# Attention and feed-forward block on one core: the opening of the kernel laid anew (constants on GpSimd, one bias load, later Wv and Wp loads, wide weight splits)

## The chip, the core and the metric
One core of one Trainium2 chip runs the whole kernel. The metric is the device time of one launch in microseconds. The kernel before takes 2347.75 us (median of 3 runs, 2345.22 to 2349.53).

## What is computed
`x` is 4 x 2048 x 512 in f32, split below into units of 512 tokens.

```
x = x + layernorm(attn(layernorm(x)))     # 16 heads of 32, causal, every 4th key is masked out
x = x + layernorm(ffn(layernorm(x)))      # one of 8 matrices, chosen by argmax(log_softmax(logits) + gumbel(u))
attn: q, k, v = y @ Wq + bq, y @ Wk + bk, y @ Wv + bv;  softmax(q k / sqrt(32)) v;  @ Wp + bp
```

Matrices and rows go through TensorE as two f16 halves each (a high part, and a low part that holds what the high part lost), with power-of-two scales taken from the largest weight, so that a projection is three f16 products for every 128 rows of the contraction.

## The kernel before
**Units.** There are 16 units (4 sequences x 4 blocks of 512 tokens). A unit normalises four row blocks (r = 0 to 3, 128 rows each), turns them by a DMA transpose, projects q, k and v, and then goes through four groups g of four heads: the largest score of each query ("peak", on DVE), its transfer into the scores as a shift, scores, exponentials (ACT), values ("pv") and sums. Then come the output projection, its norm, the feed-forward projection and its norm.

**Order.** Nothing is scheduled on the chip. The class `Order` gives each engine (PE, ACT, DVE, GpSimd, SP) a list of steps before the program is built. Each step has a rank, a duration in ns, the steps that it needs and the banks or buffers that it takes; a planner runs them forwards and backwards several times and keeps the shortest plan. An engine works through its own list strictly in order, and stands still at a step that waits for a semaphore. A changed duration, need or rank in `startup` can so move steps anywhere in the program, in all 16 units.

**The opening** (`Order.startup`, and the engine blocks of `sandwich_block`):

- SP loads (`load_w`, L738) and the row blocks (`load_x`, L719): Wk, x0, x1, Wq, x2, x3, Wv, a table of masks, Wp and the output bias, in that order. x0 to x2 take 2 or 3 transfers each, since their rows are gathered by keys that are kept and keys that are not. `turn` (L734) is the DMA transpose of a row block. `kcopy` (L753) copies two constant rows of KST to the other three key blocks.
- ACT's list begins with `load_b` (L846 to L853): logits, u, the identity matrix, then eight loads for bq and bk (128 values each) and one for bv. Then it normalises (L886, L888) and casts (L894) row blocks. `kconst` (L866) writes 2^15 into rows 96 and 97 of KST (2 x 6144 f16). `choose` (L857 to L863) is the Ln, Ln, Exp, Ln by which the feed-forward matrix is chosen; each change of function comes with a table load. `whigh` (L875) writes the high f16 part of Wq and Wk: for each column block of 128 and each of four 128-row blocks k one instruction that also reorders the columns within the block (a head's 32 columns are spread 4 apart), so 32 instructions in all. `wlow` (L1169) does the same on DVE for the low part, 32 more. Wv, Wp and the chosen matrix are split by one instruction each (128 x 2048, L879 and L1176).
- DVE: `consts` (L981 to L987), `stats` of each row block (L1020 to L1025), `wmax` (largest weight, L1096), `bmax` (L1103), then `allmax` and `scales` (L1109 to L1162: with two small matmuls on PE, L1259 and L1263, they give each matrix its scale). `fold` 0 and 1 bring bv through Wp into the output bias, `fold` 2 (L1191 to L1208, 17 instructions) cuts both biases into three bf16 rows. The output projections and the v evacuations of unit 1 wait for `fold` 2.
- GpSimd: `rstd` (L803, the inverse root), `low` (L810, low part of a row block), `rest` (L815, low part of q or k).

A first projection on PE (L1247 to L1249) needs the two split halves of its column block and all four turned row blocks.

Of the kernel before, what the change touches and what calls it, by code (L numbers as in the profile page):

```python
# [52 lines left out]
class Order:  # L53
# [69 lines left out]
    def startup(self):  # L123
        add = self.add
        add("dve", -100, 1200, ("consts",))
        add("act", -100, 7500, ("load_b",))
        for i, n in enumerate((1, 0, 2, 3)):
            add("sp", -101 if n == 1 else -99 + i, (650, 650, 1300, 1300)[i], ("load_w", n))
            add("hbm", -100 + i, (2100, 2100, 2700, 2900)[i], ("land", n), [("sp", "load_w", n)])
        add("hbm", -101, 2500, ("land", "b"), [("act", "load_b")])  # L130
        add("dve", -97, 200, ("ident",), [("act", "load_b"), ("dve", "consts")])
        add("act", -99, 5400, ("kconst",), [("dve", "consts")])
        add("sp", 0.5, 1950, ("kcopy",), [("act", "kconst")])
# [24 lines left out]
        add("dve", 0.5, 3200, ("fold", 2), [("dve", "fold", 1), ("dve", "wlow", 3), ("dve", "wlow", 4), ("dve", "scales", 2)])  # L158
# [308 lines left out]
def sandwich_block(nc, x, Wq, bq, Wk, bk, Wv, bv, Wp, bp, Wf, bf, logits, uni, cf, cb, out):  # L467
# [21 lines left out]
    with ctx:  # L489
# [42 lines left out]
        WX = sb("WX", [8, 1], F32)  # L532
        WD = sb("WD", [8, 8], F32)
# [26 lines left out]
        a_p, a_k, a_w, a_n, a_c, a_h, a_e, a_o, a_m, a_q, a_v, a_y = (  # L560
            sem(n) for n in ("a_p", "a_k", "a_w", "a_n", "a_c", "a_h", "a_e", "a_o", "a_m", "a_q", "a_v", "a_y"))
        v_p, v_c, v_w, v_f, v_ln, v_n, v_m, v_s, v_o, v_t = (
            sem(n) for n in ("v_p", "v_c", "v_w", "v_f", "v_ln", "v_n", "v_m", "v_s", "v_o", "v_t"))
        g_ln, g_p, g_q, g_s, g_o, g_r = (sem(n) for n in ("g_ln", "g_p", "g_q", "g_s", "g_o", "g_r"))
# [16 lines left out]
        BIAS = 9 * 16  # L581

        def counted(steps, signals):

            total, value = {}, {}
            for s in steps:
                name, n = signals(s)
                if n:
# [9 lines left out]
                                           {"load_b": (None, 0), "choose": ("p", 4), "kconst": ("k", 1),  # L598
                                            "whigh": ("w", 4 if s[0] == "whigh" and s[1] < 2 else 1), "exp": ("e", 1),
# [3 lines left out]
            "allmax": ("p", 2), "scales": ("p", (16, 12, 6)[s[-1]] if s[0] == "scales" else 0), "wlow": ("w", 4 if s[0] == "wlow" and s[1] < 2 else 1),  # L603
# [3 lines left out]
            "rstd": ("ln", 1), "low": ("p", 1), "rest": ("q", 1), "add": ("s", 1),  # L607
# [89 lines left out]
        def _(e):  # L697
# [6 lines left out]
            for s in order.sp:  # L704
# [45 lines left out]
                elif kind == "kcopy":  # L750
                    sp.wait_ge(a_k, 1)
# [89 lines left out]
        def _(e):  # L841
            ac = Lean(e)
            for s in order.act:
                kind = s[0]
                if kind == "load_b":
                    e.dma_start(g8(0), logits[None, :]).then_inc(d_lg, 16)  # L846
                    e.dma_start(g8(1), uni[None, :]).then_inc(d_lu, 16)
                    e.dma_start(IDF, cf).then_inc(d_cf, 16)
                    for n, b in enumerate((bq, bk)):
                        for k in range(4):  # L850
                            e.dma_start(BIA[:, n, k:k + 1], b[128 * k:128 * k + 128].rearrange("(a d) -> d a", a=4),
                                        allow_slow_non_contiguous=True).then_inc(d_b, 16)
                    e.dma_start(BIA[:, 2, :], bv.rearrange("(k p) -> p k", p=128),  # L853
                                allow_slow_non_contiguous=True).then_inc(d_b, 16)
# [9 lines left out]
                elif kind == "kconst":  # L864
                    ac.wait_ge(v_c, READY)
                    e.activation(KST[96:98, :, 0:384],  # L866
                                 ONES[96:98, 0:1].rearrange("p (a n) -> p a n", a=1).broadcast_to([2, H, 384]),
                                 ACT.Copy, scale=SM).then_inc(a_k, 1)
# [103 lines left out]
        def _(e):  # L972
# [5 lines left out]
            for s in order.dve:  # L978
# [184 lines left out]
                elif kind == "wlow":  # L1163
                    n = s[1]
                    if n < 2:
                        c = slice(128 * s[2], 128 * s[2] + 128)
                        for k in range(4):
                            dv.wait_ge(a_w, AC["whigh", n, s[2]] - 3 + k)
                            e.scalar_tensor_tensor(out=WL[:, n, k, c].rearrange("p (d a) -> p a d", a=4),  # L1169
                                                   in0=stage[n][:, k, c].rearrange("p (a d) -> p a d", a=4),  # L1170
                                                   scalar=SW[:, n:n + 1],
                                                   in1=WH[:, n, k, c].rearrange("p (d a) -> p a d", a=4),
                                                   op0=ALU.mult, op1=ALU.subtract).then_inc(v_w, 1)
# [38 lines left out]
        def _(e):  # L1212
            pe = Lean(e)
            for s in order.pe:
# [72 lines left out]
                elif kind == "score":  # L1287
# [4 lines left out]
                    pe.wait_ge(a_k, 1)  # L1292
# [37 lines left out]


_INS = ['L0_attn_x', 'L0_attn_Wq', 'L0_attn_bq', 'L0_attn_Wk', 'L0_attn_bk', 'L0_attn_Wv', 'L0_attn_bv',
        'L0_attn_Wp', 'L0_attn_bp', 'L0_ffn_W', 'L0_ffn_b', 'L0_ffn_logits', 'L0_ffn_u']


# [33 lines left out]
```

## Time and profile before

| what | value |
|---|---|
| three runs | 2345.22, 2347.75, 2349.53 us |
| the profiled execution | 2347.21 us |
| its span on the core | 2345.4 us |
| PE busy | 2255.9 us, 96% |
| ACT, DVE, GpSimd busy | 1739.0, 1629.9, 1553.1 us |
| mean granted TensorE clock | 0.99 |

The span is what the trace covers; the execution's own time is 1.8 us more. A granted clock of 1.00 is 2.4 GHz, 0.50 is 1.2 GHz. Busy shares are means over the span, and the opening is 2 to 5% of it.

### The profile page before, as it was taken

What the parts mean: (1) busy time and instruction counts of PE and PEld (TensorE: products, weight loads), DVE (VectorE), ACT (ScalarE), POOL (GpSimd) and SP (SyncE); (2) the same over time, 40 slices, a digit from 0 to 9 for tenths busy, and PEclk for the clock granted to TensorE, in tenths of its full rate; (3) what the DMA queues carried; (4) which work ended last, traced back from release to release, by engine and by line L of the source; (5) the groups of instructions that cost most, each with busy time, mean ns of one, the idle gap of its engine ahead of it and who ended that gap; (6) DMA issues with size and microseconds to landing.
All of it is one profiled execution on the core that took longest, in us unless ns stands there. A gap on an engine that the chain in (4) does not pass through costs nothing.

```text
span 2345.4 us, 43402 instructions
## 1 busy us (share of the span) xinstructions
PE 2255.9 (96%) x14996; PEld 960.0 (41%) x14996; DVE 1629.9 (69%) x4773; ACT 1739.0 (74%) x3206; POOL 1553.1 (66%) x1440
## 2 busy tenths in 40 slices
PE   4799999999999999999999999999999999999996
PEld 2344443443444444443344444443344444444422
DVE  8768667775477777677366777777727677767774
ACT  7568678688777868678876867868777686776773
POOL 3246587688655758688854747868965476777734
PEclk9899999999999999999999999999999999999998
DMA  7313122012233213112133412201223231310101
GB/s 195 79 40 91 32 51 72 17 42 69 53 96 83 59 29 70 49 40 66 39 70 81 92 31 61 67 23 36 62 56 91 61 91 30 62 49 24 35 10 41
DMA packets 224358, 137.49 MB, mean 59 GB/s; under 512 B 146730, under 2 KB 196618, under 8 KB 224138
## 3 DMA queue, kind: packets, MB, share of 16 engines
q1 hardware_dynamic: 222310, 134.65, 23.3%
q8 instruction: 118, 1.93, 0.4%
q14 instruction: 102, 0.84, 0.1%
q10 hardware_dynamic: 1828, 0.07, 0.1%
HBM read 39.69 MB, written 16.78 MB: 24 GB/s over the span
## 4 chain that ended last, share of the span: by engine, by line
PE 69%; issue 8%; DVE 7%; POOL 7%; ACT 6%; DMA 1%; SPq 1%; POOLq 0%; ACTq 0%; DVEq 0%
PE acc L1276 12%; PE acc L1312 11%; PE acc L1296 11%; PE acc L1247 9%; PE acc L1248 8%; PE acc L1249 8%; PE acc L1327 6%; POOL P L824 5%; ACT P L962 4%; PE acc L1300 2%; DVE acc L1039 2%; DVE STA L1020 1%; PE acc L1252 1%; DVE MP L1043 1%; DMA XB<-in_L_attn_x_dram 1%
## 5 line engine op out<-in xcount | busy, mean ns | idle before, releaser
L962 ACT ACTIVATE P<-acc,EX 128x512 f32<-128x512 f32 (+2 forms) x1920 | 1076.7, 639 | 229.7 <-PE acc L1300 100.2
L824 POOL TENSOR_TENSOR P<-P 128x512 f32<-128x512 f32 x732 | 907.4, 1277 | 112.8 <-PE acc L1312 86.6
L1043 DVE TENSOR_REDUCE MP<-acc 128x1 f32<-128x512 f32 (+1 forms) x1088 | 720.0, 680 | 210.3 <-PE acc L1276 206.8
L1039 DVE CUSTOM_DVE_ANT_0 acc<-acc,CB 128x96 f32<-128x96 f32 (+7 forms) x1024 | 450.8, 456 | 244.6 <-PE acc L1276 240.0
L1276 PE MATMUL acc<-KST,QST 96*128 96x512 f16 (+9 forms) x2112 | 594.6, 334 | 13.2 <-DVE MP L1039 4.5
L1296 PE MATMUL acc<-QST,KST 98*128 98x512 f16 (+2 forms) x1920 | 581.4, 354 | 15.8 <-DVE MP L1039 7.2
L1312 PE MATMUL acc<-P,V 128*32 128x512 f32 (+2 forms) x3840 | 430.5, 543 | 2.4 <-ACT P L962 2.2
L1276 PEld LDWEIGHTS acc<-KST,QST 96*128 96x128 f16 x2112 | 196.8, 98 | 302.1 <-issue 56.8
L1296 PEld LDWEIGHTS acc<-QST,KST 98*128 98x128 f16 x1920 | 182.5, 98 | 287.5 <-issue 75.2
L803 POOL TENSOR_TENSOR RR<-RR,NHALF 128x1 f32<-128x1 f32 x256 | 143.1, 563 | 202.9 <-DVE NM L1025 202.5
L1327 PE MATMUL acc<-P,ONES 128*32 128x512 f32 (+2 forms) x2304 | 231.8, 501 | 1.7 <-ACT P L962 1.6
L815 POOL TENSOR_TENSOR QKL<-SC,QKH 128x384 f16<-128x384 f32 (+1 forms) x128 | 134.7, 1052 | 136.5 <-ACT QKH L937 136.5
L1247 PE MATMUL acc<-XT,WH 128*128 128x384 f16 (+1 forms) x512 | 182.3, 356 | 12.9 <-DVE WL L1169 11.3
L1249 PE MATMUL acc<-XT,WH 128*128 128x384 f16 (+1 forms) x512 | 181.3, 354 | 0.0
L1248 PE MATMUL acc<-XT,WL 128*128 128x384 f16 (+1 forms) x512 | 181.2, 354 | 0.0
L1312 PEld LDWEIGHTS acc<-P,V 128*32 128x32 f32 x3840 | 102.8, 109 | 184.2 <-issue 145.1
L1300 PE MATMUL acc<-CB 128*128 128x176 bf16 x768 | 176.1, 241 | 0.0
L828 POOL TENSOR_TENSOR OTL<-SC,OTH 128x512 f16<-128x512 f32 x64 | 74.3, 1161 | 144.3 <-ACT OTH L969 144.0
L1039 DVE DVE_READ_ACCUMULATOR2_ANT MP<- 128x1 f32 x1024 | 144.6, 141 | 0.0
L1327 PEld LDWEIGHTS acc<-P,ONES 128*32 128x32 f32 x2304 | 70.4, 109 | 134.5 <-issue 113.5
L886 ACT ACTIVATE NM<-NM,RR 128x1 f32<-128x1 f32 x244 | 72.1, 296 | 71.1 <-POOL RR L803 67.5
L1076 DVE STREAM_TRANSPOSE SC<-acc 128x512 f32<-128x512 f32 x64 | 45.7, 714 | 112.3 <-PE acc L1327 112.3
(151 smaller groups left out, 2896.9 us busy)
## 6 DMA issues: line engine op xcount, KB each, us to landing
QST<-QKH SPq DMA_DIRECT2D x128, 128.0 KB, 3.2
XR<-in_L_attn_x_dram SPq DMA_DIRECT2D x60, 256.0 KB, 2.7
out_dram<-XR SPq DMA_DIRECT2D x60, 256.0 KB, 2.2
KST<-QKH SPq DMA_DIRECT2D x128, 96.0 KB, 2.7
XB<-in_L_attn_x_dram SPq DMA_DIRECT2D x48, 252.0 KB
QST<-QKL SPq DMA_DIRECT2D x64, 128.0 KB, 3.3
KST<-QKL SPq DMA_DIRECT2D x64, 96.0 KB, 2.7
XB<-in_L_attn_x_dram SPq DMA_DIRECT2D x20, 256.0 KB, 3.4
```

Source lines behind the costliest of these rows:

```text
L824: e.tensor_tensor(P[:, acc, a, :], P[:, acc, a, :], P[:, buf, a, :], ALU.add).then_inc(g_s, 1)
L962: e.activation(P[:, p_buf[u, g, sb_], a, t0:512], bank(*step)[:, t0:512], ACT.Exp, scale=EX[:, 1:2]).then_inc(a_e, 1)
L1039: e.tensor_tensor_reduce(out=ps, in0=ps, in1=MASKM[:, 512 - n:512], scale=1.0, scalar=-3.0e38, op0=ALU.add, op1=ALU.max, accum_out=maxima( ...
L1043: e.tensor_reduce(maxima(u, g)[:, r, a, ci:ci + 1], bank(*s)[:, 0:n], AX.X, ALU.max).then_inc(v_m, 1)
L1247: e.matmul(o, lh, rh, start=kt == 0, stop=False)
L1248: e.matmul(o, ll, rh, start=False, stop=False)
L1249: i = e.matmul(o, lh, rl, start=False, stop=kt == 3 and bias is None)
L1276: i = e.matmul(bank(*s)[:, 0:n], QST[0:96, h, 128 * r:128 * r + 128], KST[0:96, h, c0:c0 + n], start=True, stop=True)
L1296: i = e.matmul(bank(*s)[:, t0:512], KST[0:98, h, 128 * sb_:128 * sb_ + 128], QST[0:98, h, t0:512], start=True, stop=dg < 0)
L1300: i = e.matmul(bank(*s)[:, t0:t0 + MW], IDB, MASKT[dg], start=False, stop=True)
L1312: i = e.matmul(bank("pv", u, g, 0)[32 * a:32 * a + 32, t0:512], V[:, vb, 32 * h:32 * h + 32], P[:, p_buf[u, g, sb_], a, t0:512], start=fir ...
L1327: i = e.matmul(bank("sum", u, g, blocks[0])[32 * a:32 * a + 32, t0:512], ONES[:, :], P[:, buf, a, t0:512], start=sb_ == blocks[0], stop=sb ...
```

## The change
The planner's table of the opening gets new durations and needs, and the code follows it:

- The constant rows of KST are written by GpSimd, as the first step of its list, by one memset. SP's `kcopy` and PE's scores wait for GpSimd's semaphore.
- The host lays the biases out as one 128 x 3 x 4 array, and Wq and Wk with their columns already reordered. ACT issues 4 loads where it issued 12, the identity first. A one-element activation after them makes the first table load come early.
- Loads of Wv and Wp (and what goes with them) wait in SP's list until all four row blocks of unit 0 are turned.
- `whigh` and `wlow` of Wq and Wk take one instruction for each column block (128 x 4 x 128), 8 + 8 in place of 32 + 32.
- `fold` 2 is planned at 8500 ns, not at 3200.

```diff
     def startup(self):
-        add("act", -100, 7500, ("load_b",))
+        add("act", -100, 2700, ("load_b",))
         for i, n in enumerate((1, 0, 2, 3)):
-            add("sp", -101 if n == 1 else -99 + i, (650, 650, 1300, 1300)[i], ("load_w", n))
+            add("sp", -101 if n == 1 else -99 + i, (650, 650, 1300, 1300)[i], ("load_w", n),
+                [("sp", "turn", 1, 0, r) for r in range(4)] if n > 1 else [])
-        add("act", -99, 5400, ("kconst",), [("dve", "consts")])
-        add("sp", 0.5, 1950, ("kcopy",), [("act", "kconst")])
+        add("gp", -101, 5400, ("kconst",))
+        add("sp", 0.5, 1950, ("kcopy",), [("gp", "kconst")])
-                add("act", at + m, 1170, ("whigh", n, m), [("dve", "scales", 0)])
-                add("dve", at + m, 1140, ("wlow", n, m), [("act", "whigh", n, m)])
+                add("act", at + m, 620, ("whigh", n, m), [("dve", "scales", 0)])
+                add("dve", at + m, 640, ("wlow", n, m), [("act", "whigh", n, m)])
-        add("dve", 0.5, 3200, ("fold", 2), ...)
+        add("dve", 0.5, 8500, ("fold", 2), ...)
...
@@ gpsimd
-                if kind == "rstd":
+                if kind == "kconst":
+                    e.memset(KST[96:98, :, 0:384], SM).then_inc(g_k, 1)
+                    gp.wait_ge(g_k, 1)
+                elif kind == "rstd":
@@ scalar, load_b
+                    e.dma_start(IDF, cf).then_inc(d_cf, 16)
+                    e.dma_start(BIA[:, :, :], bias).then_inc(d_b, 16)
                     e.dma_start(g8(0), logits[None, :]).then_inc(d_lg, 16)
                     e.dma_start(g8(1), uni[None, :]).then_inc(d_lu, 16)
-                    e.dma_start(IDF, cf).then_inc(d_cf, 16)
-                    for n, b in enumerate((bq, bk)):
-                        for k in range(4):
-                            e.dma_start(BIA[:, n, k:k + 1], b[...].rearrange("(a d) -> d a", a=4), ...)
-                    e.dma_start(BIA[:, 2, :], bv.rearrange("(k p) -> p k", p=128), ...)
+                    ac.wait_ge(v_c, 1)
+                    e.activation(WARM[:, :], ONES[:, 0:1], ACT.Identity)
@@ scalar, whigh (wlow on DVE likewise)
-                        for k in range(4):
-                            e.activation(WH[:, n, k, c].rearrange("p (d a) -> p a d", a=4),
-                                         stage[n][:, k, c].rearrange("p (a d) -> p a d", a=4), ACT.Copy,
-                                         scale=SW[:, n:n + 1]).then_inc(a_w, 1)
+                        e.activation(WH[:, n, :, c],
+                                     stage[n][:, :, c], ACT.Copy,
+                                     scale=SW[:, n:n + 1]).then_inc(a_w, 1)
@@ kernel, on the host
+    for n, name in enumerate(('L0_attn_bq', 'L0_attn_bk')):
+        bias[:, n, :] = inputs[name].reshape(4, 4, 32).transpose(2, 1, 0).reshape(128, 4)
+    bias[:, 2, :] = inputs['L0_attn_bv'].reshape(4, 128).T
+        if name in ('L0_attn_Wq', 'L0_attn_Wk'):
+            a = a.reshape(512, 4, 4, 32).transpose(0, 1, 3, 2).reshape(512, 512)
```

**Where the lists move.** ACT's list from its 7th row, before. Line 886 is the first norm, 866 `kconst`, 875 the 32 splits; `choose` (857 to 863) stands after them:

```order
L886 ACT_TABLE_LOAD
L886 ACTIVATE NM<-NM,RR 128x1
L888 ACTIVATE XB<-XB,NM,RR 128x512
L894 ACTIVATE XP<-XB 128x512
L866 ACTIVATE KST<-ONES 2x16x384
```

The same place in the changed kernel, where 855 is the one-element activation, 858 to 864 are `choose` and 881 is the first norm:

```order
L855 ACT_TABLE_LOAD
L855 ACTIVATE WARM<-ONES 128x1
L858 ACT_TABLE_LOAD
L858 ACTIVATE XR<-XR 1x8
L860 ACTIVATE XR<-XR 1x8
L862 ACT_TABLE_LOAD
L862 ACTIVATE XR<-XR 1x8
L864 ACT_TABLE_LOAD
L864 ACTIVATE XR<-XR 1x1
L881 ACTIVATE NM<-NM,RR 128x1
```

The choice of the feed-forward matrix moved ahead of all four norms, and `kconst` left ACT.

SP's list after the first loads of x, before (738 to 742 the weights, masks and output bias, 734 the transposes, 753 `kcopy`):

```order
L738 DMA P<-in_L_attn_Wv_dram 128x4x512
L740 DMA CB<-in_cb_dram 128x1168
L738 DMA V<-in_L_attn_Wp_dram 128x4x512
L742 DMA V<-in_L_attn_bp_dram 128x512
L734 DMA_TRANSPOSE XT<-XP 128x8x128
L719 DMA XB<-in_L_attn_x_dram 126x1x512
L719 DMA XB<-in_L_attn_x_dram 2x512
L753 DMA KST<-KST 2x16x384 x3
L734 DMA_TRANSPOSE XT<-XP 128x8x128
L719 DMA XB<-in_L_attn_x_dram 1x512
```

And now, from the load of Wq on (739 the weights, 735 the transposes, 754 `kcopy`):

```order
L739 DMA P<-in_L_attn_Wq_dram 128x4x512
L754 DMA KST<-KST 2x16x384 x3
L735 DMA_TRANSPOSE XT<-XP 128x8x128
L720 DMA XB<-in_L_attn_x_dram 126x1x512
L720 DMA XB<-in_L_attn_x_dram 2x512
L735 DMA_TRANSPOSE XT<-XP 128x8x128
L735 DMA_TRANSPOSE XT<-XF 128x8x128 x2
L739 DMA P<-in_L_attn_Wv_dram 128x4x512
L741 DMA CB<-in_cb_dram 128x1168
L739 DMA V<-in_L_attn_Wp_dram 128x4x512
```

The four transposes stand closer together and ahead of Wv and Wp, the wait for the constants stands ahead of all four, and the eight transfers of x stand ahead of Wk and Wq but for the last of them.

DVE's list where `fold` 2 begins, before (1039 is a peak of group 1, 1191 to 1208 are `fold` 2):

```order
L1039 ISA acc,MP<-acc,CB 128x192
L1039 ISA MP 128x1
L1191 RECIPROCAL RC<-CO 128x2
L1198 TENSOR_SCALAR V<-V,RC 65x512
L1202 CAST R<-V 1x512
```

And in the changed kernel (1047 to 1054 close the peaks of group 2, 1185 on is `fold` 2; 1084, the output of group 0, follows its last row):

```order
L1047 TENSOR_REDUCE acc<-MP 128x16
L1052 TENSOR_SCALAR MHL<-acc 128x4x4
L1054 SCALAR_TENSOR_TENSOR MHL<-acc,MHL 128x4x4
L1185 RECIPROCAL RC<-CO 128x2
L1192 TENSOR_SCALAR V<-V,RC 65x512
```

`fold` 2 moved behind the peaks of groups 1 and 2. All other lists are laid anew too, through all 16 units, with the same kinds of steps.

## Rows read from the trace of the kernel before

**Rows 1.** The page: busy time of each engine, and the granted clock in 40 slices

```profile
PE 2255.9 (96%) x14996; PEld 960.0 (41%) x14996; DVE 1629.9 (69%) x4773; ACT 1739.0 (74%) x3206; POOL 1553.1 (66%) x1440
PEclk9899999999999999999999999999999999999998
```

**Rows 2.** Stretches: length, busy of PE, PEld, DVE, ACT, POOL, clock, DMA share, GB/s

```profile
5.00:10.00 5.00, 0.00 (x0) 0.00 (x0) 2.13 (x5) 0.31 (x1) 0.56 (x1) 1.00 1.08 307
...
80.00:87.00 7.00, 0.97 (x4) 0.26 (x3) 6.50 (x17) 0.69 (x1) 0.00 (x0) 0.50 0.33 76
87.00:100.00 13.00, 12.58 (x99) 6.61 (x98) 11.35 (x55) 9.33 (x19) 3.41 (x4) 0.76 0.36 63
...
200.00:2200.00 2000.00, 1982.85 (x13286) 845.89 (x13288) 1389.11 (x4072) 1514.53 (x2798) 1410.17 (x1299) 1.00 0.23 56
```

**Rows 3.** Timeline of PE: start, length, what [idle before <-releaser]

```profile
31.22 0.48 PE L1247 MATMUL acc<-XT,WH 128*128 128x384 f16 x1 [11.30 <-DVE WL L1169]
...
86.68 0.61 PE L1296 MATMUL acc<-QST,KST 98*128 98x512 f16 x1 [6.03 <-DVE MP L1039]
```

**Rows 4.** Timeline of ACT in the opening

```profile
9.69 1.28 ACT L886 ACT_TABLE_LOAD   x1 [9.69 <-POOL RR L803]
...
12.81 5.32 ACT L866 ACTIVATE KST<-ONES 2x6144 f16<-2x6144 f32 x1
...
18.16 0.29 ACT L886 ACTIVATE NM<-NM,RR 128x1 f32<-128x1 f32 x1
...
19.87 0.28 ACT L886 ACTIVATE NM<-NM,RR 128x1 f32<-128x1 f32 x1
...
23.25 9.64 ACT L875 ACTIVATE WH<-P,SW 128x128 f16<-128x128 f32 x32
...
36.50 1.28 ACT L857 ACT_TABLE_LOAD   x1
...
41.17 0.20 ACT L863 ACTIVATE XR<-XR 1x1 f32<-1x1 f32 x1
```

**Rows 5.** Timeline of DVE in the opening

```profile
14.45 0.69 DVE L1020 BATCH_NORM_STATS2 STA<-XB 128x6 f32<-128x512 f32 x1
...
15.51 2.28 DVE L1096 TENSOR_REDUCE WM<-P 128x1 f32<-128x2048 f32 x1
...
20.16 1.12 DVE L976 TENSOR_SCALAR PW<-WMA 128x2 int32<-128x2 int32 x1
...
25.12 0.15 DVE L1162 TENSOR_SCALAR EX<-EX 128x1 f32<-128x1 f32 x1
...
42.09 0.17 DVE L976 TENSOR_SCALAR PW<-WMA 128x2 int32<-128x2 int32 x1
...
48.18 2.34 DVE L1176 SCALAR_TENSOR_TENSOR WL<-P,SW,WH 128x2048 f16<-128x2048 f32 x1
```

**Rows 6.** Chain of waits: DVE's first four splits of Wk

```profile
26.34 1.27 DVE WL L1169 x4
```

**Rows 7.** Timeline of GpSimd: a low part

```profile
20.10 1.15 POOL L810 TENSOR_TENSOR XP<-XB,XP 128x512 f16<-128x512 f32 x1 [3.94 <-ACT XP L894]
```

**Rows 8.** Timeline of SP: how long it issues loads of x and transposes

```profile
1.27 3.43 SPq L719 DMA_DIRECT2D XB<-in_L_attn_x_dram  x5
...
5.20 1.83 SPq L719 DMA_DIRECT2D XB<-in_L_attn_x_dram  x3
...
26.41 2.61 SPq L734 DMA_TRANSPOSE XT<-XF  x2
```

**Rows 9.** DMA issues of the first 30 us: KB each, median us to landing

```profile
V<-in_L_attn_Wp_dram SPq DMA_DIRECT2D x1, 1024.0 KB, 11.9
...
YX<-in_cf_dram ACTq DMA_DIRECT2D x1, 64.0 KB, 5.1
...
XT<-XF SPq DMA_TRANSPOSE x2, 3.5
```

**Rows 10.** Timeline of DVE: first and last of the 17 rows of `fold` 2

```profile
76.60 0.16 DVE L1191 RECIPROCAL RC<-CO 128x2 f32<-128x2 f32 x1
...
85.70 0.42 DVE L1202 CAST R<-YX 1x512 bf16<-1x512 f32 x1
```

More of the change, by code:

```diff
@@ L157, in startup @@
         add("dve", 0.3, 600, ("fold", 1), [("pe", "fold"), ("hbm", "land", "b")])
-        add("dve", 0.5, 3200, ("fold", 2), [("dve", "fold", 1), ("dve", "wlow", 3), ("dve", "wlow", 4), ("dve", "scales", 2)])
+        add("dve", 0.5, 8500, ("fold", 2), [("dve", "fold", 1), ("dve", "wlow", 3), ("dve", "wlow", 4), ("dve", "scales", 2)])
     def moments(self, k, u, r, rank, after):
@@ L464, in wait_ge, with sandwich_block @@
             self.seen[sem.name] = value
-def sandwich_block(nc, x, Wq, bq, Wk, bk, Wv, bv, Wp, bp, Wf, bf, logits, uni, cf, cb, out):
+def sandwich_block(nc, x, Wq, Wk, Wv, bias, Wp, bp, Wf, bf, logits, uni, cf, cb, out):
     F32 = mybir.dt.float32
@@ L597, in sandwich_block @@
                                             "f": ("y", 1)}[s[1][0]] if s[0] == "evac" else
-                                           {"load_b": (None, 0), "choose": ("p", 4), "kconst": ("k", 1),
-                                            "whigh": ("w", 4 if s[0] == "whigh" and s[1] < 2 else 1), "exp": ("e", 1),
+                                           {"load_b": (None, 0), "choose": ("p", 4), "whigh": ("w", 1), "exp": ("e", 1),
                                             "ohigh": ("o", 1), "shift": ("m", 1), "high": ("h", 1), "cast": ("c", 1), "norm": ("n", 2)}[s[0]]))
@@ L602, in sandwich_block @@
             "choose": ("p", 4 if s[-1] else 2), "consts": ("c", 7), "ident": ("c", 1), "wmax": ("p", 1), "bmax": ("p", 3),
-            "allmax": ("p", 2), "scales": ("p", (16, 12, 6)[s[-1]] if s[0] == "scales" else 0), "wlow": ("w", 4 if s[0] == "wlow" and s[1] < 2 else 1),
+            "allmax": ("p", 2), "scales": ("p", (16, 12, 6)[s[-1]] if s[0] == "scales" else 0), "wlow": ("w", 1),
             "fold": ("f", 17 if s[-1] == 2 else 1), "stats": ("ln", 4), "norm": ("n", 1),
@@ L606, in sandwich_block @@
         GP = counted(order.gp, lambda s: {
-            "rstd": ("ln", 1), "low": ("p", 1), "rest": ("q", 1), "add": ("s", 1),
+            "kconst": ("k", 1), "rstd": ("ln", 1), "low": ("p", 1), "rest": ("q", 1), "add": ("s", 1),
             "olow": ("o", 1), "add_x": ("r", 1), "add_y": ("r", 1)}[s[0]])
@@ L863, in _ @@
                     e.activation(G8[0:1, 6, 1:2], G8[0:1, 6, 0:1], ACT.Ln).then_inc(a_p, 1)
[L864 to L868, printed above, removed]
                 elif kind == "whigh":
@@ L1166, in _ @@
                         c = slice(128 * s[2], 128 * s[2] + 128)
[L1167 to L1173, printed above, removed]
+                        dv.wait_ge(a_w, AC["whigh", n, s[2]])
+                        e.scalar_tensor_tensor(out=WL[:, n, :, c],
+                                               in0=stage[n][:, :, c],
+                                               scalar=SW[:, n:n + 1],
+                                               in1=WH[:, n, :, c],
+                                               op0=ALU.mult, op1=ALU.subtract).then_inc(v_w, 1)
                     else:
@@ L1348, in give @@
         args.append(nc.dram_tensor(f"in_{name}_dram", a.shape, _mybir.dt.from_np(a.dtype), kind="ExternalInput").ap())
+    bias = _np.zeros((128, 3, 4), _np.float32)
+    for n, name in enumerate(('L0_attn_bq', 'L0_attn_bk')):
+        bias[:, n, :] = inputs[name].reshape(4, 4, 32).transpose(2, 1, 0).reshape(128, 4)
+    bias[:, 2, :] = inputs['L0_attn_bv'].reshape(4, 128).T
     for name in _INS:
-        give(name, _np.ascontiguousarray(inputs[name]))
+        a = bias if name == 'bias' else inputs[name]
+        if name in ('L0_attn_Wq', 'L0_attn_Wk'):
+            a = a.reshape(512, 4, 4, 32).transpose(0, 1, 3, 2).reshape(512, 512)
+        give(name, _np.ascontiguousarray(a))
     BIG = -1.0e38
```

21 lines of the change are left out of this document (9 added, 12 removed).

## The prediction

> **What bounds the kernel now.** I began with the page. PE is busy 96% of the span, at a granted clock near the upper level in every slice [rows 1]. In the 2000 us from 200 to 2200 it is busy 1982.85 us, so 17 us are idle there [rows 2]: in the steady part PE's own work sets the pace. What can be won by touching the opening is therefore the time in which PE has nothing to do at the start, one for one, since whatever starts earlier there lets the same PE work begin earlier.
>
> The timeline of PE shows how much that is. Its first projection starts at 31.22 us, and later it stands 6.03 us before the matmul at 86.68 [rows 3]. The stretches show the second place again: from 80 to 87 us PE is busy 0.97 us, and the granted clock is 0.50, the lower level (1.2 GHz); from 87 to 100 it is still 0.76 [rows 2].
>
> What is waited for at 31.22? The row names DVE's split (L1169), but the first splits of Wk end at 27.61 [rows 6], 3.6 us earlier. The other input is the turned rows: two transposes are issued from 26.41 to 29.02, so the second at about 27.7, and one takes 3.5 us to land [rows 8, 9], which gives 31.2. So the turned rows come last, and the splits would be next, 3.6 us behind them at most. Behind the turned rows stands ACT: after the first cast it writes the constants for 5.32 us, and only at 18.16 does the second norm begin [rows 4].
>
> At 86.68 the cause is `fold` 2: its 17 rows run from 76.60 to 86.12 on DVE [rows 10], and the peaks of group 1 stand behind it. PE's list runs into a peak with no free bank, and the scores that are ready stand behind that peak.
>
> **Term 1, the first projection.** I walk both inputs through the new lists.
>
> *ACT and the rows.* Twelve loads become four. I price the four at 1.75 us of issue from 0.76 us, by the nearest issue rows (SP: 3.43 us for five, 1.83 for three [rows 8], so 0.6 to 0.7 each at most, 2.8 us as the upper end). u is then issued by about 2.5. Its landing is not shown by itself; I take the identity's 5.1 us [rows 9], though that one travelled beside a megabyte of weights, so u is there at 7.6 at the latest. `choose` runs from its first table load to its last activation in 41.37 - 36.50 = 4.87 us [rows 4], so it ends at 12.5; the first table load (1.28 us) that stood at 9.69 is now hidden in the wait for u. A norm with its cast takes 19.87 - 18.16 = 1.71 us, four of them 6.8, so to 19.3. GpSimd's low part adds 1.15 [rows 7], the last transpose goes out at about 20.6 and lands 3.5 later: 24.1. SP is free by then. Its issues of x and two weights are over at about 7 us, the three copies of constants need some 2 us more, the first transpose is due at 15.4, and each takes 1.3.
>
> *DVE and the scales.* About 2.1 MB (x and Wk) must land for the last `stats`, and 3.1 MB with Wq. At 307 GB/s [rows 2], from 1.6 us on, that is 8.4 and 11.7 us; small transfers at the front make it slower, say 10.5 and 14. One `stats` takes 1.06 us (14.45 to 15.51 [rows 5]), so these are done at 11.6. The second part of `choose` on DVE waits for ACT until 12.5 and takes 0.8: 13.3. Two maxima of 2.28 us [rows 5] end at 17.9, with Wq landed well before it is wanted. From the end of the second maximum (17.79) to the end of the scales (25.27) DVE took 7.5 us. Three instructions in it were held up beside GpSimd's low parts: L976 took 1.12 us at 20.16 and 0.17 at 42.09 [rows 5], its second use and a bias scaling were slowed by as much again, and `choose` took 0.3. In the new order the low parts overlap less with this; I subtract the full 3.1 and get 22.3, or 25.4 if nothing changes. One `stats` more: 23.4. The first wide split of DVE: a quarter of the 128 x 2048 split's 2.34 us [rows 5], so 0.6; the upper end is the 1.27 us of four narrow ones [rows 6]. 24.0.
>
> Both inputs come at 24, so **the first projection starts at 24.1 in place of 31.2: 7.1 us.** The ends: 22.5, if u lands in 2 us, and 27, if it lands in 7 or DVE keeps its holds. ACT's splits (9.64 us for 32 [rows 4], now 8 of about 0.6) keep ahead of DVE's.
>
> *Edits that cost nothing.* The memset on GpSimd has no row of its own. The nearest is the same write on ACT, 5.32 us; the ends are 0.5, and 13.8 by a low part's 1.15 us for 512 elements [rows 4, 7]. I take 5.3: it ends at 6, when the first `rstd` is wanted at 6 to 7, and norms wait for `choose` until 12.5 anyway. Without that cover each us past 12 would delay all rows by one. The GPSIMD Engine Reference of the Trainium skill (section 3.1) gives 1.03 to 1.8 cycles for an element in tight loops; an estimate from that page is 5.3 to 9.2 us, and by it the sum would stay as it is. No row shows such a memset.
>
> **Term 2, the rest of the opening.** `fold` 2 now comes after the peaks of groups 1 and 2. While it runs PE holds scores, values and sums of two groups and the projections of unit 1. That removes the wait of 6.03 us and part of the slow clock: 12.58 us busy at 0.76 [rows 2] would be 9.6 at 1.00, so 3 us. Against it, 9.5 us of DVE work do not vanish, and the output of group 0 waits behind them. The ends are a gain of 9 (6 + 3) and a loss of 3.5, if PE stood through all 9.5. **I take 3.5 us of gain**, nearer to the middle of what can be lost or won.
>
> The loads of Wv and Wp start at about 22 us. In PE's list the bias fold with Wp stands after three projections (8.4 us), so at 32.5; 2.4 MB at 307 GB/s land by 30. I cost them at nothing; if Wp took 11.9 us as before [rows 9], it would land at 35.1 and cost 2.6.
>
> **Term 3, all that follows.** The lists of 16 units are laid anew with the same work. I take 0, with 6 us to either side: a third of the 17 us idle of 200 to 2200 [rows 2].
>
> **Sum.** Against the profiled execution's 2347.2 us: 7.1 + 3.5 = 10.6 less, 2336.6. The median of the runs is 0.5 higher, so the forecast is 2337.
>
> **Rivals.**
>
> *Held port (0.07).* The memset is slow and holds what DVE shares with GpSimd. For it speaks the L976 row: 1.12 us against 0.17, and it ended at 21.28, when GpSimd's low part ended at 21.25 [rows 5, 7]. DVE's cast of the identity, second in its new list, would stand until a memset of 13.8 us ends at 14.3. Then 5.9 us of `stats` and small work, 4.6 of maxima, 4.4 of scales, 1.6 to the first split: the first projection at 30.8, term 1 worth 0.4, and the time 2343.8. Against it: ACT wrote the same in 5.32, and with that the cast is free at 6 and the walk above is unchanged. The rule is that of "SBUF — State Buffer" in the Trainium skill, section "Who interferes with whom": whoever issues first gets the shared ports for the whole instruction, and an f32 cast can be such a one. The trace agrees for L976; whether a memset holds them no row shows.
>
> *Won early, given back (0.09).* Late weights cost 2.6, `fold` 2 at its new place takes all of term 2 (3.5), and the q and k spreads, now in the middle of the loads of Wv, Wp and the chosen matrix, land 1.5 us later each at two steps (3). 10.6 - 9.1 leaves 1.5: 2346. For it: the DMA queues ran at a share above 1 from 5 to 10 us [rows 2].
>
> *A worse draw of the order (0.06, slower).* Place: units 2 to 14. PE stands before peaks and scores that wait for DVE and ACT; 17 us in 2000 are little, and another plan may have twice as much or more. It decides from 10.6 us on; at 2.2 times (21 more) the time is 2358. Against it: needs, buffers and all durations outside the opening are as they were.
>
> *More than forecast (0.08).* Term 2 is worth all 9, term 1 as above, a little more behind it: 2331 or below.
>
> **Numbers.** The forecast case has 0.70. A measurement of this kernel can tell about 0.2%, 4.7 us, from no change, so faster means below 2343.0. Faster: 0.70 + 0.08 and a little of the second rival, 0.80. Same: 0.14. Slower: 0.06. The range takes in term 1 from 22.5 to 27, both ends of term 2 in part and term 3: 2328 to 2345.
>
> **What would show it.** Term 1: PE's first L1247 row at 24 (its new line 1241), second norm on ACT at about 14, one table load before 5 us, memset of 5 to 6 us. Term 2: no PE wait over 3 us between 60 and 100, clock above 0.8 there, and `fold` 2 (9.5 us) after the peaks of group 2. Term 3: PE idle from 200 to 2200 of 17 us, give or take 6. The forecast is wrong if the memset is over 12 us, if PE stands at the bias fold, or if that last idle time has grown by 10.

## The result, and the profile after

The changed kernel takes **2334.35 us** (median of 5 runs, 2333.48 to 2335.92), the kernel before 2346.92 in the same comparison (2344.98 to 2349.53). The ratio is 0.9948, with a 95% interval from 0.9933 to 0.9962: faster by 12.6 us, where 10.6 were forecast and 2337 us predicted, within the range. The profiled executions span 2345.4 and 2332.1 us, 13.3 apart.

The page's busy times and granted clock, which answer to [rows 1]:

```profile
PE 2254.5 (97%) x14996; PEld 960.9 (41%) x14996; DVE 1625.2 (70%) x4749; ACT 1729.6 (74%) x3182; POOL 1558.6 (67%) x1441
PEclk9899999999999999999999999999999999999998
```

The stretches, columns as in [rows 2], with two more (31 to 50 and 70 to 80):

```profile
31.00:50.00 19.00, 14.23 (x59) 6.62 (x58) 12.70 (x37) 10.72 (x18) 6.59 (x8) 0.82 0.93 242
...
70.00:80.00 10.00, 8.63 (x38) 4.40 (x38) 8.97 (x52) 6.85 (x11) 2.31 (x2) 0.50 0.33 77
80.00:87.00 7.00, 6.75 (x49) 2.24 (x47) 5.59 (x17) 5.24 (x11) 0.66 (x2) 0.77 0.41 64
87.00:100.00 13.00, 12.52 (x105) 5.90 (x109) 11.67 (x31) 9.40 (x20) 4.16 (x4) 1.00 0.29 78
200.00:2200.00 2000.00, 1982.53 (x13286) 847.23 (x13282) 1386.71 (x4065) 1519.40 (x2803) 1417.89 (x1308) 1.00 0.22 56
```

PE's idle time, length less busy in such stretches, says where the 13.3 us went:

| stretch | before | after |
|---|---|---|
| to the first projection (31.2, 25.3) | 30.0 | 24.1 |
| from there to 200 us | 18.7 | 11.6 |
| 200 to 2200 | 17.15 | 17.47 |
| 2200 to the end | 23.6 | 24.4 |
| PE busy, whole span | 2255.9 | 2254.5 |

So about 6 us came before the first projection, 7 behind it, and the steady part gave and took nothing. PE at three places (it answers to [rows 3]):

```profile
25.26 0.48 PE L1241 MATMUL acc<-XT,WH 128*128 128x384 f16 x1 [4.39 <-DVE WL L1163]
...
45.15 0.42 PE L1270 MATMUL acc<-KST,QST 96*128 96x96 f16 x3 [4.77 <-DMA QST<-QKL]
...
104.12 0.34 PE L1270 MATMUL acc<-KST,QST 96*128 96x384 f16 x1 [1.40 <-DVE SC L1084]
```

Of the wait of 6.03 us nothing is left: from 80 to 87 PE is busy 6.75 us in place of 0.97. The wait at 45.15 is for the spread of the first q (the DMA copies of its high and low part into QST, from which the scores read it; L768); the chain of waits gives it 8.9 us from issue to landing:

```profile
36.21 8.90 DMA QST<-QKL
```

The kernel before had a wait of this kind as well, for the spread of the second q and not of the first:

```profile
59.43 0.24 PE L1276 MATMUL acc<-KST,QST 96*128 96x96 f16 x1 [3.62 <-issue]
```

The row names no releaser, but the same matmul in *e1_wide* (below), which has the same order, does:

```profile
59.64 0.24 PE L1274 MATMUL acc<-KST,QST 96*128 96x96 f16 x1 [4.36 <-DMA QST<-QKL]
```

So the longest wait for a q spread is 4.77 us now and was 3.62: it moved from the second q to the first and grew by 1.2 us.

ACT, as in [rows 4]: the first table load stands at 2.63 us, `choose` ends at 8.99, the first two norms start at 8.90 and 10.60, and seven wide splits take 4.40 us:

```profile
2.63 1.28 ACT L855 ACT_TABLE_LOAD   x1 [2.63 <-issue]
...
8.90 0.28 ACT L881 ACTIVATE NM<-NM,RR 128x1 f32<-128x1 f32 x1
...
21.78 4.40 ACT L870 ACTIVATE WH<-P,SW 128x512 f16<-128x512 f32 x7 [5.54 <-DVE CO L1120]
```

DVE, as in [rows 5]; the first two rows are long and end together, at 6.03 and 6.02, and the later MAX8 is the same instruction on the same shape:

```profile
2.52 3.51 DVE L985 CAST IDH<-YX 128x128 f16<-128x128 f32 x1 [0.47 <-DMA YX<-in_cf_dram]
4.34 1.68 DVE L989 MAX8 XR<-XR 1x8 f32<-1x8 f32 x1
...
12.62 0.69 DVE L1015 BATCH_NORM_STATS2 STA<-XB 128x6 f32<-128x512 f32 x1 [2.93 <-DMA XB<-in_L_attn_x_dram]
...
14.13 0.16 DVE L999 MAX8 XR<-XR 1x8 f32<-1x8 f32 x1
...
14.48 4.45 DVE L1091 TENSOR_REDUCE WM<-P 128x1 f32<-128x2048 f32 x2
...
21.10 0.17 DVE L971 TENSOR_SCALAR PW<-WMA 128x2 int32<-128x2 int32 x1
...
24.38 3.39 DVE L1163 SCALAR_TENSOR_TENSOR WL<-P,SW,WH 128x512 f16<-128x512 f32 x5
...
92.31 0.16 DVE L1185 RECIPROCAL RC<-CO 128x2 f32<-128x2 f32 x1
```

GpSimd's memset, and SP's transposes with what stands around them ([rows 8] had 2.61 us for the last two; now 2.98, all issued by 22.6):

```profile
0.73 5.21 POOL L801 MEMSET KST<- 2x6144 f16 x1 [0.29 <-POOLq L1337]
```

```profile
15.49 1.36 SPq L735 DMA_TRANSPOSE XT<-XP  x1
...
18.33 1.26 SPq L735 DMA_TRANSPOSE XT<-XP  x1
19.64 2.98 SPq L735 DMA_TRANSPOSE XT<-XF  x2
22.66 0.59 SPq L739 DMA_DIRECT2D P<-in_L_attn_Wv_dram  x1
```

### The profile page after: what moved, and what is told of

The parts are those of the page before. It is cut to its first block, busy times and chain, and to the rows that moved or that the text cites. A ratio compares the mean times of both kernels' runs of the same rounds, so it can differ in the third digit from the quotient of the medians.

```text
span 2332.1 us, 43387 instructions
## 1 busy us (share of the span) xinstructions
PE 2254.5 (97%) x14996; PEld 960.9 (41%) x14996; DVE 1625.2 (70%) x4749; ACT 1729.6 (74%) x3182; POOL 1558.6 (67%) x1441
## 3 DMA queue, kind: packets, MB, share of 16 engines
q1 hardware_dynamic: 222310, 134.65, 22.6%
## 4 chain that ended last, share of the span: by engine, by line
PE 72%; issue 7%; POOL 7%; ACT 6%; DVE 6%; DMA 1%; SPq 1%; ACTq 0%; POOLq 0%; DVEq 0%
PE acc L1270 12%; PE acc L1306 12%; PE acc L1290 11%; PE acc L1241 9%; PE acc L1242 9%; PE acc L1243 9%; PE acc L1321 6%; POOL P L828 4%; ACT P L957 3%; PE acc L1294 2%; DVE acc L1034 1%; DVE MP L1038 1%; PE acc L1246 1%; POOL XP L814 1%; POOL RR L807 1%
## 5 line engine op out<-in xcount | busy, mean ns | idle before, releaser
L1290 PE MATMUL acc<-QST,KST 98*128 98x512 f16 (+2 forms) x1920 | 580.9, 354 | 12.6 <-ACT P L957 5.6
L1015 DVE BATCH_NORM_STATS2 STA<-YX 128x6 f32<-128x512 f32 x126 | 86.6, 687 | 31.8 <-ACT YX L921 16.9
```

The lines of the kernel that those rows point to most:

```text
L1290: i = e.matmul(bank(*s)[:, t0:512], KST[0:98, h, 128 * sb_:128 * sb_ + 128], QST[0:98, h, t0:512], start=True, stop=dg < 0)
```

## The experiments

Each run is compared with the kernel before on the same chip; its medians were 2348.16 us beside the four e runs, 2348.84 beside g1_sp, g2_spw, f4_draw and f5_plan3200 (on another chip), 2349.29 beside u1_spback, f2_x3first, f3_spread and h1_both. Where lists are edited, that is done behind the planner's last step, so nothing else moves.

**One part at a time, in the order of before.** *e1_wide*: the wide splits alone.

```diff
-                        for k in range(4):
-                            e.activation(WH[:, n, k, c].rearrange("p (d a) -> p a d", a=4), ...
+                        e.activation(WH[:, n, :, c], stage[n][:, :, c], ACT.Copy, ...
```

> The kernel before with one part of the change: wide splits of Wq and Wk (8 + 8 instructions), every list in the order of before. Theory (the turned rows come last at 31.2 us): PE's first projection stays between 30.7 and 31.5 us, though the first split of Wk ends at 27.0 or earlier; the time stays within 1.5 us of before, 2346.9. Rival (the splits set the start, as the releaser in the row says): first projection at 27 to 28.5, time 3 to 4 us less.

2346.72 us, ratio 0.9992 (0.9983 to 1.0001): no change that can be told from none. Its PE, then its DVE (first wide splits of Wk):

```profile
31.03 0.48 PE L1245 MATMUL acc<-XT,WH 128*128 128x384 f16 x1 [11.23 <-DMA XT<-XF]
```

```profile
25.93 0.74 DVE L1167 SCALAR_TENSOR_TENSOR WL<-P,SW,WH 128x512 f16<-128x512 f32 x1
```

The first split ends at 26.67, 0.9 us earlier than in [rows 6] and 4.4 us ahead of PE, which starts as before: there the turned rows come last, although the row of [rows 3] named the split.

*e2_gpconst*: the memset alone, at the head of GpSimd's list.

```diff
+order.act.remove(("kconst",))
+order.gp.insert(0, ("kconst",))
```

> The kernel before with the KST constants written by a memset at the head of GpSimd's list in place of the 5.3 us activation; all else in the order of before. Theory (ACT's 5.3 us stood in the way of the turned rows): the second norm begins at 12.8 instead of 18.2, the rows are turned by about 26, and the first projection starts at 27.5 to 28 with DVE's narrow split as the new last input, so 3 to 4 us less: 2343 to 2344. Rival (SP's own queue holds the transposes, not ACT): first projection still after 30 us and less than 1 us gained.

2347.15 us, ratio 0.9994 (0.9985 to 1.0003), first projection at 31.20. My theory fell, the rival held. The trace shows why. First GpSimd's low parts, then SP:

```profile
12.54 1.16 POOL L815 TENSOR_TENSOR XP<-XB,XP 128x512 f16<-128x512 f32 x1 [0.17 <-ACT XP L894]
15.76 1.16 POOL L815 TENSOR_TENSOR XP<-XB,XP 128x512 f16<-128x512 f32 x1
...
18.32 1.15 POOL L815 TENSOR_TENSOR XF<-XB,XF 128x512 f16<-128x512 f32 x1 [0.29 <-ACT XF L894]
```

```profile
13.73 3.23 SPq L736 DMA_TRANSPOSE XT<-XP  x1
17.01 1.34 SPq L721 DMA_DIRECT2D XB<-in_L_attn_x_dram  x2
18.40 2.16 SPq L755 DMA_DIRECT2D KST<-KST  x3
20.60 3.23 SPq L736 DMA_TRANSPOSE XT<-XP  x1
23.88 2.01 SPq L721 DMA_DIRECT2D XB<-in_L_attn_x_dram  x3
25.94 3.25 SPq L736 DMA_TRANSPOSE XT<-XF  x2
```

All four rows are ready at 19.5 us, and the last transposes still go out at 25.94: SP issues without a gap from 13.7 on, 5.5 us of it loads and copies that stand between the transposes. Behind the turned rows stood SP's own list. ACT's 5.3 us lay beside it: in the kernel before, SP waited for ACT's late row only from 20.75 to 21.28.

*e3_fold*: `fold` 2 alone, behind the peaks of group 2.

```diff
+order.dve.remove(("fold", 2))
+order.dve.insert(order.dve.index(("peaks", 0, 2)) + 1, ("fold", 2))
```

> The kernel before with the one step fold 2 (17 DVE instructions) moved in DVE's list from within the peaks of group 1 to behind the peaks of group 2, nothing else. Theory (its old place made PE stand 6.0 us at a low clock): no PE wait over 3 us between 76 and 95 us, PE idle between 31 and 120 us falls from 16.9 to 11 or less, and the time falls by 4 to 8 us: 2339 to 2343. Rival (9.5 us of DVE work cost the same wherever they stand): a PE wait of 5 us or more appears near the new place and the time stays within 1.5 us of 2346.9.

2352.57 us, ratio 1.0020 (1.0011 to 1.0029): slightly slower. The wait goes from 86.7 and comes back:

```profile
112.31 0.42 PE L1278 MATMUL acc<-KST,QST 96*128 96x288 f16 x1 [7.59 <-DVE MP L1041]
```

Here `fold` 2 begins at 102.58, and PE, which began its next projections at 99.1, is through with what it can run at 104.7. In the changed kernel `fold` 2 begins at 92.31, and PE has projections, values and sums until 102.7.

*e4_three*: the three edits above together.

> The kernel before with the three parts together (wide splits, constants on GpSimd, fold 2 behind the peaks of group 2), in the order of before otherwise; biases still in nine loads, choice of the matrix late, Wv and Wp loaded early. Theory (opening parts explain the change, the new order of the other units does not): first projection at 25.5 to 27, time 8 to 11 us less than before, 2336 to 2339. Rival (a lucky new order of the 16 units carries the change): 5 us less at most, 2342 or above.

2350.35 us, ratio 1.0010 (1.0001 to 1.0019); first projection at 30.92, waiting for the turned rows again, and the wait of 7.59 us behind `fold` 2 again, at 111.67. The three parts of the change that lie on the engines bring nothing while SP's list and the rest of the order are those of before.

**SP's list.** *g1_sp* is before with the wide splits, the memset, and the copies of constants and three of the four row blocks of unit 1 moved behind the fourth transpose; *g2_spw* moves the loads of Wv and Wp (with the masks and bp) there too.

```diff
+at = order.sp.index(("turn", 1, 0, 3))
+late = [("kcopy",)] + [("load_x", 1, r) for r in (1, 2, 3)]
+late = [("load_w", 2), ("load_w", 3)] + late          # g2_spw only
+late = [s for s in late if order.sp.index(s) < at]
+order.sp[:] = [s for s in order.sp[:at + 1] if s not in late] + late + order.sp[at + 1:]
```

> The kernel before with wide splits and the constants on GpSimd, and in SP's list the constant copies and the loads of x1 to x3 of unit 1 moved behind the fourth transpose; Wv and Wp still loaded early; everything else in the order of before. Theory now (what kept the rows from being turned was SP's own list, where a transpose that is ready stood behind 1.3 to 2.2 us pieces of other issue, and each transpose took 3.2 us to issue while the weights were landing): transposes at 13.7, 18.3, then back to back; last one lands at 25 to 28 us, so the first projection starts at 25 to 28 in place of 31.2. Rival (the landing of Wv and Wp alone holds the transposes up): first projection after 29.

> The same with the loads of Wv, masks, Wp and output bias also behind the fourth transpose. Theory (landing weights lengthen a transpose's issue from 1.3 to 3.2 us): all four issues below 1.7 us, rows turned by 23 us, and the first projection bound by DVE's first split at 24.5 to 25.3, so 6 us earlier than before. For the time: if what is won at the start passes to the end one for one, 2341 to 2343; rival (in lists that were not planned for it PE only waits longer further on): less than 2.5 us gained, 2345 or above, with PE idle of 31 to 200 us grown by 3 us or more over 18.9.

g1_sp: 2342.34 us, ratio 0.9971 (0.9961 to 0.9981). g2_spw: 2337.03 us, ratio 0.9953 (0.9940 to 0.9966). PE and SP of g1_sp:

```profile
26.55 0.48 PE L1249 MATMUL acc<-XT,WH 128*128 128x384 f16 x1 [5.65 <-DMA XT<-XF]
```

```profile
14.59 3.09 SPq L740 DMA_TRANSPOSE XT<-XP  x1
...
19.12 2.11 SPq L740 DMA_TRANSPOSE XT<-XP  x1
21.28 2.86 SPq L740 DMA_TRANSPOSE XT<-XF  x2
```

And of g2_spw:

```profile
24.94 0.50 PE L1250 MATMUL acc<-XT,WH 128*128 128x384 f16 x1 [4.31 <-DVE WL L1172]
...
80.66 0.61 PE L1299 MATMUL acc<-QST,KST 98*128 98x512 f16 x1 [6.05 <-DVE MP L1043]
```

```profile
14.44 1.38 SPq L741 DMA_TRANSPOSE XT<-XP  x1
...
18.75 2.74 SPq L741 DMA_TRANSPOSE XT<-XF  x2
```

With SP's list mended beside the two engine edits the first projection comes 4.7 us earlier, and with the weights behind the transposes 6.3; there DVE comes last, as in the changed kernel. g2_spw has the twelve bias loads and the late `choose` of before, and its first projection is even 0.3 us ahead of the changed kernel's 25.26: those two parts of the change are not needed for it. The wait for `fold` 2 is untouched.

SP's list mended without the engine edits was not run. In the kernel before, the fourth row's low part is ready at 24.67:

```profile
23.49 1.18 POOL L810 TENSOR_TENSOR XF<-XB,XF 128x512 f16<-128x512 f32 x1 [0.54 <-ACT XF L894]
```

A transpose of g2_spw lands 3.2 to 3.5 us after its issue, so an estimate for SP's list alone is 27.9 to 28.2, some 3 of the 6.3 us; the rest would need the engine edits.

g2_spw's time was better than said (2341 to 2343). Its profiled execution, 2341.49 us, was the slowest of six, and in it PE's idle time up to 200 us is 42.9, 5.8 less than before. For the rest of the 11.8 us between the medians no trace shows a place.

*u1_spback* asks the same from the other side: the changed kernel with the pattern of SP's list of before around the turned rows, all else left. It is not the old list to the row: eight transfers of x and the three copies, 7.1 us of issue, stand between its transposes, where five and three with 5.8 us stood before, and one transfer stands ahead of the fourth.

```diff
+early = [("load_w", 2), ("load_w", 3)]
+between = [("kcopy",)] + [("load_x", 1, r) for r in (1, 2, 3)]
+order.sp[:] = [s for s in order.sp if s not in early + between]
+at = order.sp.index(("turn", 1, 0, 0))
+order.sp[at:at] = early
...
```

> The changed kernel with SP's list of before restored around the turned rows alone: Wv, the masks, Wp and bp ahead of the first transpose, the copies of the scale constant and the x loads of unit 1 between the transposes. Memset on GpSimd, wide splits, bias load and fold 2's place stay. Theory (SP's list carries the gain at the first projection): transposes are issued in about 3 us each instead of 1.3 and land in 7 to 8 us instead of 3.3 to 4.1, the last is issued at 24 to 27 us, the first projection starts at 29 to 32 us [<-DMA XT<-XF] instead of 25.3, and the time is 4 to 7 us above the changed kernel's 2334.35: 2338 to 2341. Rival (the memset, the warm table and the early first norm carry it): first projection within 1.5 us of 25.3 and the time within 2 us of the changed kernel's.

2338.42 us, ratio 0.9956 (0.9942 to 0.9970). PE, then SP:

```profile
34.68 0.48 PE L1249 MATMUL acc<-XT,WH 128*128 128x384 f16 x1 [13.75 <-DMA XT<-XF]
```

```profile
26.73 3.34 SPq L743 DMA_TRANSPOSE XT<-XF  x1
...
30.74 1.24 SPq L743 DMA_TRANSPOSE XT<-XF  x1
```

SP's list does hold the first projection, and by more than I had said: 34.7 us, 9.4 later than in the changed kernel and 3.5 later than before, part of which is the longer list. Yet the time is only 4.1 us above the changed kernel's median (and 3.6 to 5.8 above the three variants of it that ran on the same chip, below), and 10.9 below that of before. The windows say why. PE's idle time between the first projection and 200 us is 11.6 us in the changed kernel and 6.8 here (40.3 up to 200 us, less 33.5 ahead of 34.68): with the later start the wait of 4.8 us for q's spread is gone. Against the 18.7 us of before, the new order holds 11.9 behind a first projection that is 3.5 later; 8.4 remain, and the profiled spans are 8.0 apart.

Do the two parts add up? One is SP's list in the old order, with two engine edits that are worth nothing by themselves (g2_spw). The other is the new order with the old pattern on SP, which keeps the engine edits, the bias load and the early `choose` (u1_spback). By the medians they bring 11.8 and 10.9 us, and both together 12.6, so most of the one would be absorbed by the other. By PE's idle time up to 200 us they bring 5.8 and 8.5, and both together 13.1, which is nearly a sum. The two measures differ mainly by the 6 us of g2_spw's median that its trace does not show, so how far the parts overlap is **open**.

**What sets `fold` 2's place, and the draw.** *f5_plan3200* gives `fold` 2 its old planned time, *f4_draw* another one near the new, which shakes the order.

```diff
-        add("dve", 0.5, 8500, ("fold", 2), ...
+        add("dve", 0.5, 3200, ("fold", 2), ...    # f5_plan3200; f4_draw: 8400
```

> The changed kernel with one number of the planner put back: fold 2 at 3200 ns, not 8500; the code that runs in each step is that of the change, all lists are laid anew. Theory (a step costs PE nothing where the planner knows its length, since it then lays other work under it): fold 2 stands among peaks again, PE has a wait of 4 us or more at its end, and the time is 3 to 6 us above the changed kernel, 2338 to 2341. Rival (the place of fold 2 is a matter of chance, and the early start gives the 12.5 us): 2333 to 2336.

> The changed kernel with fold 2 planned at 8400 ns in place of 8500: no step changes, but the lists are another draw of the planner. It measures how far a new draw alone moves the time. Theory (draws differ little, since the steady part idles 17 us in all of them): within 3 us of the changed kernel, 2331.5 to 2337.5. Rival (a lucky draw is part of the 12.5 us): 2338 or above.

2333.86 us, ratio 0.9941 (0.9928 to 0.9954), and 2333.83 us, ratio 0.9940 (0.9926 to 0.9954): both the changed kernel's time. With 3200 `fold` 2 still comes behind the peaks of group 2, at 88.49 us; with 8400 it comes at 80.82, among the peaks of later groups and ahead of the output of group 0, and the longest PE wait from 50 to 140 us is 1.88. The number 8500 is not what moved it, and its exact place is worth nothing measurable once the rest of the opening is laid anew. Nor is the wait behind it gone in every draw. In f5_plan3200 `fold` 2 ends at 99.10, the output of group 0 follows it, and PE stands for that:

```profile
99.90 0.34 PE L1241 MATMUL acc<-XT,WH 128*128 128x384 f16 x1 [4.29 <-DVE SC L1071]
```

PE's idle time up to 200 us is 34.8 us there all the same, against 35.6 in the changed kernel: this draw idles less elsewhere. The three draws of the order lie within 1 us of each other.

**The two waits left.** *f2_x3first* loads the last row block ahead of Wk; *f3_spread* puts two residual loads and one of x behind q's spread; *h1_both* does both.

```diff
+order.sp.remove(("load_x", 0, 3))                                # f2_x3first
+order.sp.insert(order.sp.index(("load_w", 1)), ("load_x", 0, 3))
+for late in (("load_r", 0, 0), ("load_r", 0, 1), ("load_x", 1, 3)):   # f3_spread
+    order.sp.remove(late)
+    order.sp.insert(order.sp.index(("spread", ("q", 0, 0))) + 1, late)
```

> The changed kernel with the load of the last row block of unit 0 moved ahead of Wk's in SP's list. Theory (the late landing of that block held the statistics, then the maxima, then the scales, and cost term 1 its missing 1.1 us): the fourth group of L1015 starts at 10 to 11 us instead of 12.6, the maxima end at 16.5 to 18 instead of 18.9, the first projection starts at 24.0 to 24.6 instead of 25.3, and the time falls by 0.5 to 1.2 us. Rival (Wk and Wq land as much later as the block lands earlier, and the maxima wait for them instead): first projection within 0.4 us of 25.3, time the same.

> The changed kernel with two residual loads and one x load of SP's list moved behind the spread of the first q (L768). Theory (q's spread lands late, 8.9 us after its issue, since transfers issued just ahead of it share the DMA engines, and the PE waits 4.8 us for it at 45.2 us): issue 1.5 us earlier, landing 6 to 8 us after issue, the wait shrinks to 0 to 3 us, and the time falls by 1.5 to 4 us. Rival (the copies of k and the spread itself, with Wf still landing, set the landing, or the wait passes on to the next spread or to the peaks): the wait stays over 3.5 us or another of the same size appears by 70 us, and the time is within 1 us of the changed kernel's.

> Both edits together, as the version that could beat both kernels. Theory (independent waits on one path): first projection at 24.0 to 24.6 us, the wait at q's spread 0 to 3 us, 2330 to 2333 us. Rival (the idle time of the first 200 us, 35.6 us in the changed kernel, is set by the DVE's work for the first peaks, and what is won ahead of it is given back there): 2333 to 2336 us.

f2_x3first: 2334.83 us, ratio 0.9936 (0.9923 to 0.9950). The rival held; its DVE shows the exchange:

```profile
9.61 0.68 DVE L1017 BATCH_NORM_STATS2 STA<-XB 128x6 f32<-128x512 f32 x1
...
13.41 2.29 DVE L1093 TENSOR_REDUCE WM<-P 128x1 f32<-128x2048 f32 x1 [1.89 <-DMA P<-in_L_attn_Wk_dram]
17.39 2.29 DVE L1093 TENSOR_REDUCE WM<-P 128x1 f32<-128x2048 f32 x1 [1.69 <-DMA P<-in_L_attn_Wq_dram]
```

The statistics are done 3 us earlier (f5_plan3200, whose plan put that block ahead of Wk by itself, shows the same, with the first projection at 25.38), and both maxima now wait for their weights and end at 19.7 instead of 18.9; the first projection is at 25.93. What comes in by 17 us is one amount of data, and whichever block is last in it holds the scales.

f3_spread: 2333.66 us, ratio 0.9933 (0.9920 to 0.9947). The wait at q's spread is 2.95 us in place of 4.77, but f4_draw, whose SP list I had not touched, shows 2.95 as well, and the time moved by less than runs differ. Inconclusive: the spread can land sooner, and what that is worth is under 2 us. h1_both: 2332.58 us (2331.13 to 2333.47), ratio 0.9930 (0.9916 to 0.9943), the lowest median of the study. Its first projection is at 26.1 (the first edit hurts), and no wait at the first q's spread is left (1.39 us idle from 31 to 50), but 3.46 us stand from 50 to 70. It is 1.8 us under the changed kernel's median, less than the 2.4 by which the medians of the kernel before differ from one group of runs to another (2346.92 to 2349.29): as fast as the changed kernel or a trifle faster, no more can be said.

## Why the prediction was right

**What bounds the kernel.** That the opening is won one for one is borne out: idle time fell by 13.1 us up to 200 us and the span by 13.3. That the turned rows came last at 31.22 is shown by e1_wide. "Behind the turned rows stands ACT" was **wrong**: e2_gpconst took its 5.32 us away and nothing moved. The right reading lay in SP's list, which I had looked at only for its ends (5 loads, 2 transposes), not for what it did between 13 and 26 us. The forecast survived since the change also mends SP's list, and my walk used the new list.

**Term 1** said 24.1 us and 7.1 of gain; measured 25.26 and 6.0. Term by term: four loads took 1.9 us of issue (said 1.75), u was there for `choose` at 4.1 (said 7.6), so the rows with their low parts were ready at 18.8 (said 20.45); the last transpose went out at 20.99 (said 20.6) and landed at most 4.1 us later, by 25.1. The row names DVE's split, which ended at the same time within 0.1 us, so both inputs came together, as I had them. The step that was short is "say 10.5 and 14", the landings of x and Wq: the last `stats` began at 12.62, the maxima ended at 18.93 (said 17.9). f2_x3first shows that this is the amount of data, and not the order of two loads. The scales took 4.4 us, as said, with L971 at 0.17 in place of 1.12. The first wide split took 0.7 (said 0.6).

**The memset** was priced at 5.3 and took 5.21, at no cost: the first `rstd` ran at 7.48, and norms were held by `choose`. An estimate from the Trainium skill's GPSIMD Engine Reference (section 3.1) had been 5.3 to 9.2 us; the trace lies just below its lower end.

**Held port.** The mechanism is there, at the smaller size. The cast of the identity took 3.51 us, to 6.03; it was 0.22 us in the kernel before, and the memset ended at 5.94. That agrees with the rule of "SBUF — State Buffer" in the Trainium skill, section "Who interferes with whom", that the one who is first gets the shared ports for its whole instruction. e2_gpconst and g1_sp have the same memset and run the cast well behind it, at 13.94 and 14.70: 0.22 us again. So it is the overlap that costs the time. DVE's own memsets beside GpSimd's were not held (the last, 128x512, took 0.48 us at 1.56, as in the kernel before). It cost nothing as far as the trace shows, since DVE stood 2.93 us for the fourth row block later anyway. No run has the cast early without the memset, so its price was not measured.

**Term 2** said 3.5 us; PE's idle time behind the first projection fell by 7.2. The sign was right, and two of the three things that I named show (no wait over 3 us from 60 to 100, and `fold` 2 behind the peaks of group 2). The third, a clock above 0.8, holds for the mean of 60 to 100 (0.83, before 0.75) and not in each part: 1.00 against 0.76 from 87 to 100, 0.77 against 0.50 from 80 to 87, but 0.50 against 0.82 from 70 to 80. The mechanism was half of it, and the size was off by a factor of two. Moving `fold` 2 alone (e3_fold) loses 4 us, and its planned time is indifferent (f5_plan3200). By the traces the wait is short where PE has work left to run beside `fold` 2 (until 102.7 us in the changed kernel) and comes back where it has not (7.59 us in e3_fold, 4.29 in f5_plan3200). That is argued from the traces; no run gave PE more or less work beside it in one and the same order. The 7.2 us also hold waits that I had given no term: from 50 to 70 us PE's idle time fell from 4.4 to 1.7, from 70 to 80 from 4.1 to 1.4. From 31 to 50 it grew from 1.2 to 4.8, by the wait for q's spread.

**The loads of Wv and Wp** at nothing: right for what I priced. The bias fold did not wait, and Wp landed 8.1 us after its issue. But I costed only their own users. Behind them and the chosen matrix, q's spread landed 8.9 us after its issue, where the spreads of the kernel before took 2.9 to 6.0, and PE stood 4.77 us, where its longest such wait had been 3.62. That is the third step of the rival "won early, given back", priced at 1.5 us later at each of two spreads. It came at one, 2.9 us later than the slowest before; its other two steps did not come. f3_spread shortens it without a clear gain, so which transfer ahead of it matters is open.

**Term 3** said 0 give or take 6; idle time from 200 to 2200 changed by 0.3 us, and the tail by 0.8. Two further draws gave the same total.

The forecast of 10.6 us so came near the 12.6 with some luck: term 1 was 1.1 us too high, term 2 was 3.7 too low, and the path behind term 1 was read wrongly.

Not tried: the changed order with `fold` 2 put back into its old place, which would price that move inside the new order; and SP's list mended alone, without the engine edits.

## What to carry to other kernels

When an input is late, read the issuing queue's list between the moment the data is ready and the moment the transfer goes out; work on an engine that runs beside a busy queue can be taken away without winning anything. Edits that bring nothing alone may be needed once the queue is mended (wide splits and memset: 1.4 and 1.0 us by the medians, neither clear of nothing; with the queue's list 11.8; the share of each in that was not measured). The gains of two improvements of one opening need not add up, so undo each from the finished kernel as well as adding it to the old one, and hold the medians against the idle time in the traces. A long step moved behind others is only hidden if the engine that waits still has work at that time.

## What was not expected of the hardware

One and the same transpose takes SP from 1.2 to 3.3 us to issue: 3.04, 2.79, 1.25 and 1.31 us in the kernel before, 1.36, 1.26, 1.31 and 1.62 in the changed kernel, 2.78, 1.61, 3.34 and 1.24 in u1_spback. It was short in all four places once Wv and Wp were behind it (g2_spw, 1.27 to 1.40) and long twice with them ahead (g1_sp, 3.09 and 2.11). That suggests the transfers in flight. Yet f2_x3first has 2.97 for its first with Wv and Wp behind, when Wk and Wq were still landing, and u1_spback has 1.61 between two long ones; so the cause is open.

A memset on GpSimd that only writes held a cast on DVE from f32 to f16 for 3.51 us. The MAX8 of eight elements behind it took 1.68 us at 4.34, against 0.16 at 14.13. It ended with the cast, so it may only have stood behind the cast in DVE's own order; no run tells the two apart.
